# The order of the wide row's transposes and the next input in a block-quantised FP4 network

## The reference

```python
def fp4_quant_dequant(x):
    xb = x.reshape(shape[:-1] + (shape[-1] // BLOCK, BLOCK))      # BLOCK = 16
    scale = jnp.max(jnp.abs(xb), axis=-1, keepdims=True) / 6.0
    scale = jnp.maximum(scale, jnp.float32(1e-12))
    xn = xb / scale
    idx = jnp.searchsorted(_MID, jnp.abs(xn))
    q = _GRID[idx] * jnp.sign(xn) * scale
    return q.reshape(shape)

gate = fp4_linear(x, w_gate)          # both operands go through fp4_quant_dequant
y = fp4_linear(x, w_up)
h = jax.nn.silu(gate) * y
return fp4_linear(h, w_down)
```

## Time and profile before

| what | value |
|---|---|
| median of 3 runs | 1109.37 us (1109.18 to 1115.99) |
| profiled execution | 1103.91 us, its span 1102.2 us |
| PE busy | 864.3 us (78%) |
| DVE busy | 770.6 us (70%) |
| ACT busy | 439.3 us (40%) |
| POOL busy | 125.7 us (11%) |
| mean granted PE clock | 0.903 |

### The profile page before, as it was taken

How to read it: one execution, slowest core, us unless ns; L and a number is a source line. 1 busy time by engine, 2 the same in 40 slices (tenths; PEclk the granted TensorE clock), 3 DMA queues, 4 the chain that set the end, 5 groups by cost and what they waited for, 6 DMA issues and landing times. The chain is left out here.

```text
span 1102.2 us, 19778 instructions
## 1 busy us (share of the span) xinstructions
PE 864.3 (78%) x7220; PEld 490.9 (45%) x7220; DVE 770.6 (70%) x1438; ACT 439.3 (40%) x788; POOL 125.7 (11%) x106
## 2 busy tenths in 40 slices
PE   5518999989988775999875847999996986567675
PEld 4216766666665541443322313443443762344443
DVE  1762344688878984999979597888884441778885
ACT  3616566656545431555433750111112247222222
POOL 4420000000000001000000980000000000043330
PEclk8859999999989986999998888999998988678878
DMA  8500000000000000355451538666560000000001
GB/s 187 80 1 2 2 3 2 2 3 2 2 2 2 2 1 1 155 199 193 168 163 68 196 137 250 193 206 209 186 196 0 1 1 1 1 10 10 19 10 29
DMA packets 54054, 79.82 MB, mean 72 GB/s; under 512 B 14352, under 2 KB 28496, under 8 KB 53840
## 3 DMA queue, kind: packets, MB, share of 16 engines
q1 hardware_dynamic: 49584, 76.57, 21.9%
q10 hardware_dynamic: 4384, 2.10, 0.7%
HBM read 40.90 MB, written 35.65 MB: 69 GB/s over the span
## 5 line engine op out<-in xcount | busy, mean ns | idle before, releaser
L1159 PE MATMUL bank<-so_g,Wd 128*128 128x512 f32 x256 | 129.1, 596 | 4.9 <-DVE so_g L1218 4.9
L1398 ACT ACTIVATE so_u<-bank,bu 128x512 f32<-128x512 f32 x128 | 87.5, 685 | 80.3 <-PE bank L57 77.6
L1218 DVE TENSOR_TENSOR so_g<-so_u,bank 128x512 f32<-128x512 f32 x128 | 84.3, 673 | 22.1 <-PE bank L1145 19.0
L903 ACT ACTIVATE att_qk<-bank 128x512 f32<-128x512 f32 x128 | 66.8, 602 | 43.4 <-PE bank L733 43.0
L991 DVE TENSOR_TENSOR att_am<-bank,causal 128x512 f32<-128x512 f32 x64 | 44.0, 688 | 47.5 <-PE bank L767 47.4
L767 PE MATMUL bank<-att_qk 64*128 64x128 f32 x1024 | 76.2, 289 | 0.0
L1499 DVE SCALAR_TENSOR_TENSOR so_made<-bank,bg,so_u 128x512 f32<-128x512 f32 x95 | 68.6, 745 | 7.0 <-DMA hidden<-so_made 5.1
L767 PEld LDWEIGHTS bank<-att_qk 64*128 64x128 f32 x1024 | 63.7, 191 | 20.2 <-issue 20.2
L1159 PEld LDWEIGHTS bank<-so_g,Wd 128*128 128x128 f32 x256 | 47.7, 191 | 54.2 <-issue 32.6
L1383 POOL TENSOR_TENSOR so_made<-so_u,so_g 128x512 f32<-128x512 f32 x33 | 48.1, 1503 | 171.4 <-DVE so_cnt L1554 170.1
L1145 PE MATMUL bank<-F,spread 128*128 (+1 forms) x128 | 47.9, 385 | 18.2 <-DMA F<-so_flo 18.2
(11 more groups left out here) (380 smaller groups left out, 1785.3 us busy)
## 6 DMA issues: line engine op xcount, KB each, us to landing
hidden<-so_made SPq DMA_DIRECT2D x128, 256.0 KB, 2.0
so_u<-hidden SPq DMA_DIRECT2D x64, 512.0 KB, 3.9
xin<-in_L_attn_x_dram ACTq DMA_DIRECT2D x8, 256.0 KB, 8.2
out_dram<-ff_ot SPq DMA_DIRECT2D x8, 256.0 KB, 2.3
so_other<-so_key SPq DMA_DIRECT2D x2, 512.0 KB, 5.6
wm<-in_L_wmod_dram SPq DMA_DIRECT2D x2, 384.0 KB, 5.8
F<-so_fhi SPq DMA_DIRECT2D x4, 128.0 KB, 4.9
F<-so_flo SPq DMA_DIRECT2D x4, 128.0 KB, 4.0
```

What stands on the lines that cost most here:

```text
L903: nc.scalar.activation(qk[t % 2][:, r, :, :].rearrange("p a l -> p (a l)"), psF[r], ACT.Relu).then_inc(s_["fe"], 1)
L1159: nc.tensor.matmul(psY[j][:, :], Wd[:, n, :], hh[n % 4][:], start=False, stop=n == EBLK - 1).then_inc(s_dn[n % 4], 1)
L1218: nc.vector.tensor_tensor(hh[k % 4][:], pg[k // 2 % 4][:, k % 2, :], psW[k % 4][:, :], ALU.mult).then_inc(s_hh[k % 4], 1)
L1398: nc.scalar.activation(u[m % NU_][:], psU[m % 3][:, :], ACT.Silu, bias=bu[:, k:k + 1], scale=1.0 / WS).then_inc(s_u, 1)
```

## The change

In turns with a following input (t = 0 to 5), PE now makes all three hidden_back() calls in a row, then quantised_back(t + 2), gate_up(t + 2, 0), gate_up(t + 2, 1) and down(t). Before, these were interleaved: block 0, the next input's transposes, block 1, first products, block 2, second products. ACT's turn is changed in the same way.

```diff
@@ PE, turn() @@
                             hidden_back(t, 0, psT)
+                            hidden_back(t, 1, psT if follow > 0 else psH)
+                            hidden_back(t, 2, psT if follow > 0 else psU[0])
                             if follow > 1:
                                 quantised_back(t + 2)
-                            hidden_back(t, 1, psT if follow > 0 else psH)
-                            if follow > 1:
                                 gate_up(t + 2, 0)
-                            hidden_back(t, 2, psT if follow > 0 else psU[0])
-                            if follow > 1:
                                 gate_up(t + 2, 1)
                             down(t)
@@ ACT, turn() @@
                             take_hidden(t, 0, psT)
+                            take_hidden(t, 1, psT if follow > 0 else psH)
+                            take_hidden(t, 2, psT if follow > 0 else psU[0])
                             if follow > 1:
                                 take_x(t + 2)
-                            take_hidden(t, 1, psT if follow > 0 else psH)
-                            if follow > 1:
                                 silu(t + 2, 0)
-                            take_hidden(t, 2, psT if follow > 0 else psU[0])
-                            if follow > 1:
                                 silu(t + 2, 1)
```

## The result

The changed kernel is a little slower: a median of 1113.68 us (20 runs, 1101.06 to 1120.55) against 1101.59 us for the kernel before (20 runs, 1096.60 to 1115.99). The ratio is 1.0076, with a 95% interval of 1.0041 to 1.0110, so +4.5 to +12 us, +8.4 us in the middle. The ratio is formed without the runs that lie more than 1.5% above the fastest of their kernel; the medians, which take in all runs, differ by 12.1 us.

The account below looks back on a forecast made before the run. It took the last stage's loop of VectorE and TensorE waits as binding, TensorE alone between xq and silu. Terms 0 - 0 - 3.05 + 5.4 = +2.3 us on the 1109.37 us median gave 1111.7 us, range 1105 to 1117 us.

Parts of the forecast that it names:

- Step 1: Blocks 1 and 2 fit into TensorE's 5.15 us gap before xq, done 1.6 us ahead of it; costs nothing.
- Rival 4: ScalarE's copies and TensorE's transposes of the hidden row run past xq, needing over 1.6 us delay; 0.05 with anything else.
- Step 2: Removing block 1's 0.85 us between xq's transposes and gate products saves 0; TensorE idles some 0.7 us for ScalarE's copy.
- Step 3: Block 2's transposes leave the stretch between first and second products: 0.85 us saved in one turn, 0.44 in five, 3.05 us.
- Step 4: The pause before the gate products delays the clock's rise by 1.8 us: 0.9 us per turn, 5.4 us in all.
- rival 1: The pause doesn't matter to the clock and only block 2's saving remains: -3.05 us, 1106.3 us; chance 0.30 with its surroundings.
- Rival 2: The shortened gap keeps the clock up, so six turns run at VectorE's floor: -13 us, 1096.2 us; chance 0.06.
- rival 3: The clock's rise is put off past the down projection in each turn: +28 us, 1137 us; chance 0.04.

Follow-up runs that it names:

- half of it: Only block 1 moved ahead of xq's transposes, block 2 left between first and second products, against the changed order, stage six times: 1966.40 us.
- the filled pause: Changed order plus one unused 128 x 192 product between xq's transposes and the gate products: 1901.87 us with six stages, ratio 0.9952 to the kernel before with one.
- the second profile: The unaltered changed kernel compared once more with the kernel before, same chip, profiled in its longest run: ratio 1.0040, 1112.08 against 1101.54 us.
- the six stages in a row: The last stage, fp4_network(), run six times in one launch: order before 1925.69 us, changed order 1942.59 us.
- the gap filled: Changed order plus unused products in TensorE's gap before xq's transposes and in the pause, against the kernel before: ratio 0.9860, then 0.9900; 1851.52 us with six stages.

## Why the prediction was right in direction and short in size

**Step 1, the cover: right.** The blocks start 1.43 and 1.45 us apart, and the wait for xq is 2.26 us in the turn shown, where 2.3 us were forecast. Rival 4, a delay past xq, fell with it.

**Step 2, block 1 leaves the chain for nothing: right.** The gate products start on the end of the xqT copy, and the pause is 0.68 us.

**Step 3, block 2 saves 0.44 to 0.85 us per turn: right, by two runs.** The whole change is 4.0 us per stage faster than half of it, and so is the filled pause against the order before, where the sum had 3.05 us. In the second of them the rest is the low stretch's 0.6 us per turn, of which half is lost time, 6 * 0.3 = 1.8 us at most.

**Step 4, the clock: the cause was right, the size per turn about right.** The cost of the pause, changed order against filled pause, is 6.8 us per stage, where the sum had 5.4. The low stretch is 5.4 - 3.4 = 2.0 us longer than with the pause filled, where 1.8 had been taken, and 1.4 us longer than with the order before. That the low stretch is 0.6 us shorter with the shorter gap was in no term. The mean clock of the six windows, forecast at about 0.71, is 0.74.

One reading behind this step was wrong. I had written that the trace had no low stretch with such a pause in this stage, and so only bounded the cost. It has one, ahead of the first turn, where the gate products of input 0 wait for xqT just so. Before:

```profile
947.55 1.54 PE L1848 MATMUL bank<-wgT,ff_xqT 128*128 128x352 f32 x2 [0.67 <-ACT ff_xqT L1917]
```
```profile
945.76:955.76 10.00, 8.91 (x20) 0.63 0.00 0
```

By 20 * (1 - c) this low stretch goes on for 7.4 us behind the start of xq's transposes, longer than any of the six in the earlier trace rows (3.0 to 6.2 us). It was a sign for the cost of the pause and against rival 1, there to be read before the change was run.

**The term that was missing** is the end. I had written that in the last two turns the edit leaves their order alone, and costed them at nothing. But the clock carries over: in the profile of after, 2.1 us of the 4.0 us of the stage are the last down projection at half clock (4.98 against 2.86 us), and 0.9 us the sixth turn. In the second profile the last piece is 39.06 us again, against 35.96 us. In five turns, the place that I had worked out with most care, the first profile shows only +0.9 us (forecast: 5 * 0.39 = 1.9 us), the second +4.3 us, and the six stages in a row +1.1 us each.

The end costs as much in the six stages in a row. From input 7 of the last stage to the end, the order before, the changed one, half of the change and the filled pause:

```profile
1887.65:1923.60 35.95, 22.62 (x82) 0.88 0.08 22
1899.31:1938.30 38.99, 27.65 (x74) 0.68 0.07 21
1927.04:1965.80 38.76, 24.74 (x78) 0.76 0.07 21
1861.12:1896.90 35.78, 22.41 (x76) 0.83 0.08 23
```

The two orders with the pause have the dear end, the two without it have not.

So of the measured +8 us, 4.0 us (first profile) to 7.4 us (second) are seen in the stage, and 3.5 us per stage in the six in a row. These 3.5 us lie within the interval of the second comparison (0 to +8.8 us) and just below that of the first (+4.5 to +12 us). Where the rest of the first comes from stays open; no run here shows any effect of the change in front of the stage.

**Rival 2** (the clock stays up) was rightly put low for this kernel: the low stretches are all there. Its price was right. With the gap filled it is 12.4 us per stage, against 13 us worked out. **Rival 1** fell with the filled pause, **rival 3** with the low stretches: the longest, 8.0 us, ends inside the down projection and not past it, and the mean is 5.3 to 6.7 us in the two profiles.

**The rule of the Trainium skill** (TensorE: Matmul & The Clock Gate, Part 4) that transposes don't count for the clock as matmuls do isn't borne out by these fp32 transposes: block 2's transposes in the pause did what the unused product of 128 x 192 did, 85.5 against 85.4 us for five turns.

## What to carry to other kernels

When TensorE comes out of an idle gap at the low clock, expect a pause before the clock has risen to cost more than its length: here 0.7 us of idleness that was hidden behind a copy, and that cost nothing on the chain by itself, cost 6.8 us in six turns and their end. Before moving work off a chain, look at what it was covering; here block 2 in the place of block 1 keeps the cover and still leaves the chain shorter. And where one engine waits for another in every turn, filling the sure part of its gap with unused products can be worth more than the order of the useful ones: here the best version of this study takes 0.986 to 0.990 of the time of the kernel before, and beats both.

## What the runs showed that I had not expected

The mean granted clock over a turn rose with the changed order (0.82 to 0.84) while the turn became longer. The clock's figure says nothing without TensorE's busy time beside it.

The piece before the stage, the same code in every kernel, ended between 938.2 and 957.4 us in single executions, 19 us apart, more than any version of this stage is worth, the one with the gap filled included (12.4 us). Six stages in one launch had runs within 3 to 10 us of each other and told the orders apart in four runs each.

The stage can settle into a beat: with the pause filled, all turns took 17.1 us with low stretches of 3.4 us; in half of the change they alternated between 19.2 and 18.2 us, with 6.8 and 4.9 us. A single profile shows one such beat, not their mean.
